# One-hot rows of slots in a graph network: formed by GpSimd from a slot table, one operation behind each gather

## What is computed

```python
edge_index = jnp.stack([src, dst])          # src, dst: 400000 each, sorted by dst
x = layernorm(x + gnn0(x, edge_index, edge_attr_4, edge_attr_8))

def sconv(x, src, dst, basis, wi, W, R, b):  # once in each of the three layers
    z = einsum('nc,kco->nko', x, W)          # 64 taps
    msg = sum over 8 corners of basis[:, s] * z[src, wi[:, s]]
    agg = segment_sum(msg, dst) / clip(cnt, 1)
    return agg + x @ R + b
```

## Time and profile before

| | |
|---|---|
| median of 3 timed runs | 15385.09 us (15372.33 to 15392.76) |
| span of the profiled execution | 20957.9 us |
| TensorE busy | 15299.0 us (73% of the span) |
| VectorE busy | 11387.0 us (54%) |
| GpSimd busy | 11380.3 us (54%), 12003 instructions |
| ScalarE busy | 3304.1 us (16%) |
| mean granted clock of TensorE | 0.788 of full speed |
| chain that ended last | TensorE 51%, another core or an unknown queue 28%, issue 14% |
| DMA | 353.06 MB, mean 17 GB/s |

### The profile page before, as it was taken

How to read it: one execution, slowest core, us unless ns; L and a number is a source line. 1 busy time by engine, 2 the same in 40 slices (tenths; PEclk the granted TensorE clock), 3 DMA queues, 4 the chain that set the end, 5 groups by cost and what they waited for, 6 DMA issues and landing times.

```text
span 20957.9 us, 179979 instructions
## 1 busy us (share of the span) xinstructions
PE 15299.0 (73%) x55111; PEld 8212.8 (39%) x55111; DVE 11387.0 (54%) x19145; ACT 3304.1 (16%) x4009; POOL 11380.3 (54%) x12003
## 2 busy tenths in 40 slices
PE   7788888888866767676666676667666676766676
PEld 3333333333333444443433343444443343434343
DVE  4556666656655555555545555555555555555555
ACT  1111111111111111111111111111111111111111
POOL 5445555555545555555545555555554555555554
PEclk7666666666678888888878888888887888888888
DMA  1000000000010000000010000000001000000000
GB/s 33 13 14 15 15 15 15 15 14 15 15 24 16 16 16 16 16 16 16 16 23 16 17 16 16 16 16 16 17 16 23 16 16 16 16 16 16 16 16 22
DMA packets 886190, 353.06 MB, mean 17 GB/s; under 512 B 604191, under 2 KB 877680, under 8 KB 885872
## 3 DMA queue, kind: packets, MB, share of 16 engines
q0 software_dynamic: 386208, 210.78, 5.9%
q1 hardware_dynamic: 329276, 112.29, 2.3%
q10 hardware_dynamic: 170644, 29.29, 0.8%
HBM read 314.88 MB, written 36.56 MB: 17 GB/s over the span
## 4 chain that ended last, share of the span: by engine, by line
PE 51%; another core or an unknown queue 28%; issue 14%; ACT 3%; DVE 3%; ACTq 1%; DMA 0%; POOL 0%; DVEq 0%; SPq 0%; POOLq 0%
PE ps L1547 17%; PE ps L1559 16%; PE ps L1459 5%; PE ps L1570 4%; PE ps L1475 3%; ACT big L792 2%; PE ps L1448 2%; PE ps L1442 2%; DVE big L1056 1%; PE ps L1432 1%; ACT big L710 1%; ACTq L802 1%; ACT big L700 0%; PE ps L1414 0%
## 5 line engine op out<-in xcount | busy, mean ns | idle before, releaser
L571 POOL DMA_INDIRECT xg<-x_rows,idx x8790 | 8316.4, 946 | 6310.6 <-DVE big L1254 3682.7
L1547 PE MATMUL ps<-big 128*128 128x256 f32 x18816 | 5050.5, 422 | 1286.7 <-ACT big L792 1250.4
L1237 DVE TENSOR_TENSOR big<-ps,onehot 128x1024 f32<-128x1024 f32 x2352 | 2864.7, 1218 | 5084.9 <-remote 3417.8
L1547 PEld LDWEIGHTS ps<-big 128*128 128x128 f32 x18816 | 3863.2, 211 | 3111.9 <-issue 2581.3
L571 POOL DMA_INDIRECT xg<-in_x,idx x3125 | 2974.6, 952 | 2806.5 <-DVE big L1026 1826.0
L1570 PE MATMUL ps<-big,w_taps 128*32 128x512 f32 x9408 | 1544.9, 734 | 3060.8 <-issue 2851.8
L792 ACT COPY big<-ps 128x1024 f32<-128x1024 f32 x2352 | 2353.5, 1013 | 8828.4 <-PE ps L1547 5318.7
L1559 PE MATMUL ps<-xw,big 128*128 128x512 f32 x8232 | 3671.5, 597 | 50.5 <-issue 23.2
L1459 PE MATMUL ps<-w,big 65*128 65x256 f32 x6272 | 2498.1, 541 | 126.9 <-DVE big L1056 85.6
L1559 PEld LDWEIGHTS ps<-xw,big 128*128 128x128 f32 x8232 | 1543.4, 190 | 2006.9 <-issue 1981.1
L1459 PEld LDWEIGHTS ps<-w,big 65*128 65x128 f32 x6272 | 1566.0, 267 | 1875.0 <-issue 1562.7
(11 more groups left out here) (139 smaller groups left out, 6620.8 us busy)
## 6 DMA issues: line engine op xcount, KB each, us to landing
xg<-x_rows,idx POOLq DMA_INDIRECT x8790
xg<-in_x,idx POOLq DMA_INDIRECT x3125
row_of<-pick_rows SPq DMA_DIRECT2D x294, 128.0 KB
agg_rows<-rts ACTq DMA_DIRECT2D x294, 64.0 KB
meta<-in_coord_t SPq DMA_DIRECT2D x294, 48.0 KB
big<-in_rad SPq DMA_DIRECT2D x196, 64.0 KB
meta<-meta_items SPq DMA_DIRECT2D x392, 32.0 KB
idx<-in_src_t SPq DMA_DIRECT2D x392, 16.0 KB
```

The costliest lines, as they stand in the source:

```text
L571: return nc.gpsimd.indirect_dma_start(out=dst_tile, out_offset=None, in_=table, in_offset=bass.IndirectOffsetOnAxis(ap=index, axis=0))
L1237: v.tensor_tensor(bm[:, ring], hat_outer[:, its].rearrange("p n c b -> p n (c b)").unsqueeze(3) .to_broadcast([P, 4, 16, J]), onehot[:, it ...
L1547: tr = nc.tensor.matmul(ps[:, 2 * (ch % 2) + r // 2, 256 * (r % 2):256 * (r % 2) + 256], xm[:, at].rearrange("p a c -> p (a c)"), bm[:, at ...
```

## The change

In the layers the one-hot rows are formed by GpSimd. Behind each gather it issues one TENSOR_SCALAR that compares the 16 slot numbers with the tile's slot, one number per partition; for tiles without a gather it issues the operation alone. That makes 32 operations of 128x16 a step, 9408 in the three layers. `onehot` gets two halves, one for each parity of steps, and the table has one channel of slots (`meta[:, par, 3]`) in place of two. The first part keeps its comparison on VectorE, without line 1038. GpSimd now waits for the step's table (`meta_loaded`) before its first gather, SyncE waits for the rows of two steps earlier (`onehot_ready`) before it loads over their table, and VectorE waits for the rows of a quarter before that quarter's first multiply. Making and storing the table takes three VectorE operations and one DMA less. `xt`, used between the layers, moves into the shared buffer `big`; the wide path is changed in the same way.

```diff
-    META = 9
+    META = 8
...
-        slot = sb("slot", [P, STEP])
-        onehot = sb("onehot", [P, STEP, CH])
+        onehot = sb("onehot", [P, 2, STEP, CH])
...
-            def load_meta(i, par, used, table, first, end):
+            def load_meta(i, par, used, table, first, end, made=0):
...
                 sp.sem_inc(loads_go, 1)
-                sp.dma_start(meta[:, par, 3:5, :], meta_items[:, ds(i, 1), 3:5, :].rearrange("p n c i -> p (n c) i")
+                if due(made):
+                    sp.wait_ge(onehot_ready, made)
+                    sp.sem_inc(loads_go, 1)
+                sp.dma_start(meta[:, par, 3:4, :], meta_items[:, ds(i, 1), 3:4, :].rearrange("p n c i -> p (n c) i")
                              ).then_inc(meta_loaded[par], 16)
...
-                    sp.dma_start(by_step[:, :, 3, :], quarter_t.rearrange("p (n i) -> p n i", i=STEP)
-                                 ).then_inc(meta_stored, 16)
-                    sp.dma_start(by_step[:, :, 4, :], place_t.rearrange("p (n i) -> p n i", i=STEP)
+                    sp.dma_start(by_step[:, :, 3, :], slot_t.rearrange("p (n i) -> p n i", i=STEP)
                                  ).then_inc(meta_stored, 16)
...
-            def gather_sources(table, phase, par, twice, group_free, rest=STEP, picked_in=()):
+            def gather_sources(table, phase, par, twice, group_free, rest=STEP, picked_in=(), with_hots=False):
                 pool.wait_ge(idx_loaded[par], 16 * phase * steps_of(path, par) + 8 * twice)
                 pool.sem_inc(gathers_go, 1)
+                if with_hots:
+                    pool.wait_ge(meta_loaded[par], 2 * loads(path, par, phase, twice))
+                    pool.sem_inc(gathers_go, 1)
                 for q in range(4):
                     if group_free:
                         pool.wait_ge(*group_free(q))
                         pool.sem_inc(gathers_go, 1)
                     for r in range(QUART):
                         s = QUART * q + r
-                        if s >= rest or q in picked_in and r == PICK:
-                            continue
-                        gather(xg[:, par, s, :], table, idx[:, par, s:s + 1]).then_inc(x_in[par][q], 16)
+                        if not (s >= rest or q in picked_in and r == PICK):
+                            gather(xg[:, par, s, :], table, idx[:, par, s:s + 1]).then_inc(x_in[par][q], 16)
+                        if with_hots:
+                            hot = nc.gpsimd.tensor_scalar(onehot[:, par, s, 0:J], slot_ids[:], meta[:, par, 3, s:s + 1],
+                                                          None, ALU.is_equal)
+                    if with_hots:
+                        hot.then_inc(onehot_ready, 1)
...
-                link(v.tensor_scalar(quarter_t.bitcast(I32), dst_i, NG.bit_length() - 1, None, ALU.arith_shift_right))
-                link(v.tensor_tensor(quarter_t, quarter_t.bitcast(I32), first_dst, ALU.subtract))
-                link(v.tensor_scalar(place_t.bitcast(I32), dst_i, NG - 1, None, ALU.bitwise_and))
-                link(v.tensor_copy(place_t, place_t.bitcast(I32)))
+                link(v.tensor_tensor(slot_t, dst_i, first_dst, ALU.subtract))
...
-                        v.scalar_tensor_tensor(slot[:], meta[:, par, 3, :], float(GROUP), meta[:, par, 4, :], ALU.mult, ALU.add
-                                               ).then_inc(dve_step, 1)
-                        at = at + MASKS
-                        dve.wait_ge(dve_step, at)
-
                         if due(i):
                             dve.wait_ge(deg_done, i)
-                        v.tensor_tensor(onehot[:, :, 0:J], slot[:].unsqueeze(2).to_broadcast([P, STEP, J]),
+                        v.tensor_tensor(onehot[:, 0, :, 0:J], meta[:, par, 3, :].unsqueeze(2).to_broadcast([P, STEP, J]),
                                         slot_ids[:].unsqueeze(1).to_broadcast([P, STEP, J]), ALU.is_equal
                                         ).then_inc(onehot_ready, 1)
...
-                v.scalar_tensor_tensor(slot[:], meta[:, par, 3, :], float(GROUP), meta[:, par, 4, :], ALU.mult, ALU.add
-                                       ).then_inc(dve_step, 1)
-                dve.wait_ge(dve_step, prior + 1)
...
-                v.tensor_tensor(onehot[:, :, 0:J], ids_ps.unsqueeze(1).to_broadcast([P, STEP, J]),
-                                slot[:].unsqueeze(2).to_broadcast([P, STEP, J]), ALU.is_equal).then_inc(dve_step, 1)
...
+                    if ch % 2 == 0:
+                        dve.wait_ge(onehot_ready, STEPS + 4 * n1 + ch // 2 + 1)
                     v.tensor_tensor(bm[:, ring], hat_outer[:, its].rearrange("p n c b -> p n (c b)").unsqueeze(3)
                                     .to_broadcast([P, 4, 16, J]),
-                                    onehot[:, its, 0:J].unsqueeze(2).to_broadcast([P, 4, 16, J]), ALU.mult)
+                                    onehot[:, par, its, 0:J].unsqueeze(2).to_broadcast([P, 4, 16, J]), ALU.mult)
```

More of the change, by code:

```diff
@@ L236, in graph_kernel @@
         picked, at = part(at, (J, CH))
+        assert at <= BIG
+        xt, at = part(TABLES_AT + 2 * NI, (2, BANK))
         assert at <= BIG
@@ L489, in l0_loads @@
                     load_indices(0, i + 1, 1 - par, twice)
-                load_meta(i, par, 0 if early and i < 2 else i - 1, sh_table, 5, META)
+                load_meta(i, par, 0 if early and i < 2 else i - 1, sh_table, 4, META)
                 load_carry(i - 1, 1 - par, 0 if early and i < 3 else i - 2)
@@ L648, in layer_gathers @@
                             else lambda q: (xm_ready[2 * q + 1], l * STEPS + i - 1))
-                    gather_sources(x_rows, l + 1, par, twice, free, padded if last else STEP, path.picks)
+                    gather_sources(x_rows, l + 1, par, twice, free, padded if last else STEP, path.picks, True)
                 for i in range(2):
@@ L684, in copy_block @@
                                ps[:, 1, :].rearrange("p (c n i) -> p c n i", c=4, n=4)).then_inc(item_out, 1)
[L685 to L687 removed]
+                nc.scalar.copy(src_t, ps[:, 2, 0:P]).then_inc(item_out, 1)
             if not path.narrow:
@@ L1011, in features @@
                     hv = xg[:, par, its, MUL:CH].rearrange("p n (u i) -> p n i u", i=3)
-                    sh0 = meta[:, par, 5, its]
-                    sh1 = meta[:, par, 6:9, its].rearrange("p i n -> p n i")
+                    sh0 = meta[:, par, 4, its]
+                    sh1 = meta[:, par, 5:8, its].rearrange("p i n -> p n i")
                     f_s = feat[:, its, :].rearrange("p n (s u) -> p n s u", s=4)
@@ L1393, in transpose_block @@
             def transpose_block(b):
-                pe.wait_ge(rows_ready, 3 * (b + 1))
+                pe.wait_ge(rows_ready, 2 * (b + 1))
                 if due(b):
-                    pe.wait_ge(item_out, 4 * b)
-                for c in range(5):
+                    pe.wait_ge(item_out, 3 * b)
+                for c in range(4):
                     nc.tensor.transpose(ps[:, c // 4, (c % 4) * P:(c % 4) * P + P], table_f[:, c * P:c * P + P],
                                         ident[:])
-                for c in range(5, META):
+                for c in range(4, META):
                     nc.tensor.transpose(ps[:, c // 4, (c % 4) * P:(c % 4) * P + P],
-                                        attr_r[:, (c - 2) * P:(c - 1) * P], ident[:])
-                nc.tensor.transpose(ps[:, 2, P:2 * P], src_f, ident[:]).then_inc(item_tr, 1)
+                                        attr_r[:, (c - 1) * P:c * P], ident[:])
+                nc.tensor.transpose(ps[:, 2, 0:P], src_f, ident[:]).then_inc(item_tr, 1)
             if not path.narrow:
@@ L1432, in l0_degrees @@
                 nc.tensor.matmul(ps[CH:2 * CH, 7, :].rearrange("p (s i) -> p i s", s=J), ones[:, 0:CH],
-                                 onehot[:, :, 0:J], start=True, stop=True, tile_position=(0, CH)).then_inc(deg_done, 1)
+                                 onehot[:, 0, :, 0:J], start=True, stop=True, tile_position=(0, CH)).then_inc(deg_done, 1)
             def first_layer(i, f):
@@ L1474, in item_sums @@
                         m = 2 * par + h
-                        tr = nc.tensor.matmul(ps[CH * m:CH * m + CH, SUMS[e % 2], :], onehot[:, 2 * q + h, :],
+                        tr = nc.tensor.matmul(ps[CH * m:CH * m + CH, SUMS[e % 2], :], onehot[:, 0, 2 * q + h, :],
                                               prod[:, q % 8, h, :], start=True, stop=True, tile_position=(0, CH * m))
```

72 lines of the change are left out of this document (31 added, 41 removed).

## The result

The changed kernel takes 18451.5 us (18444.48 to 18459.25 in 4 runs), the kernel before takes 15379.1 us (15372.33 to 15392.76 in 4 runs) beside it. The ratio is 1.1997, 95% interval 1.1982 to 1.2012: 3072 us slower. The forecast was 16786 us with a range up to 17915, so the sign was right and the time lay outside the range.

What follows compares the result with a forecast made beforehand. The prediction took GpSimd, issuing gathers nearly without a break, to bound the timed runs. 15385 us, plus 1411 for the added operations, less 10 for the first part, gave 16786 us, range 15350 to 17915.

Steps and rivals of the forecast that it cites:

- The bound, GpSimd: Whole kernel: the timed runs are GpSimd issuing gathers nearly without a break, 1.25 us apart.
- the floor of 15147 us: Whole kernel: time from GpSimd's gathers, totals, one wait, start and end alone, 98.5% of the measured median.
- the 31.5 us of the compute side: End of a layer: TensorE with its helpers needs 31.5 us a step, less than GpSimd's 37.5.
- Taking the pauses out: Every step: 14.2 us of pause, 5573 us in all, was taken to be in the profiled execution alone.
- the span hardly moves: Profile after: its span was expected within 1.5% of 20957.9 us, while the timed median grows.
- Terms (1) to (4): VectorE work removed in layers 0, removals in the first part -10 us, narrower tables 0, new waits 0.
- doesn't wait for long: Layers, VectorE's line 1237: its new wait for a quarter's last row was expected to be short and cost 0.
- Term (5): Layers, GpSimd: 9408 added operations behind gathers at 0.15 us each, mostly serial, +1411 us.
- full gap: Layers, GpSimd: each operation costs its own time and a 0.30 us gap, 0.40 in all, +3763 us; chance 0.08.
- Hidden: Layers, GpSimd: operations fit in the 0.30 us behind each gather, so not slower, 15375 us; chance 0.15.
- pipelined like a MEMSET: Layers, GpSimd: each operation costs 0.03 to 0.08 us, +282 to +753 us; chance 0.17.
- GpSimd isn't the bound: Timed runs: the 1.25 us spacing is stretched by profiling, VectorE's relief counts, 15095 to 15350 us; chance 0.04.

Runs made afterwards that it cites:

- The quiet trace: The kernel before, unchanged, run again for its profile on a chip without a pause in every step: 15362.8 us.
- the tables alone: The changed kernel with the comparison back on VectorE and no operations behind GpSimd's gathers: 15372.5 us, ratio 0.9997 to the kernel before.

## Why the prediction was right or wrong

**The bound, GpSimd: right.** The unbroken distance of 1.249, the floor of 15147 us and the 31.5 us of the compute side led to "GpSimd issues gathers nearly without a break". The quiet trace shows just that, and three times 200 us on VectorE changed nothing.

**Taking the pauses out: right in effect, wrong in its reason.** The prediction said that they are "in the profiled execution alone". They belong to some chips, where the timed runs have them too: 20696 to 21033 us. That the trace and the times ahead of the prediction came from different kinds of chip fits this, though no record names theirs. So "the span hardly moves" was wrong twice. The new profile is from a quiet chip (18449.1 us), and on a chip with pauses the span is 20338.4, 3.0% below the given 20957.9 where at most 1.5% was allowed. The reason given there, that 12.5 us of waiting in a step cover the added work, did hold: 32 x 0.33 = 10.6 us fit. That the pauses could go by it was not foreseen.

**Terms (1) to (4): right within the measurement.** VectorE's 255 us in the layers are worth 0, the tables and new waits 0. The start and the first part were taken at -10; the tables alone gave -5 us, within 15 us of 0 and of -10 alike. VectorE's first multiply does wait for GpSimd, 6465.5 us, against "doesn't wait for long". That is VectorE's spare time in another row and costs nothing, as the sum above closes without it.

**Term (5), the price of the operation: this is the step that failed.** The number of operations and "mostly serial" were right, c was not: 0.33 us instead of 0.15, 3083 us instead of 1411. The ends of the bound were 0 and 0.40, and c lies between them. The choice inside went wrong. It was made by two neighbours, a MEMSET on GpSimd (0.10) and a 128x16 copy on VectorE (0.18). The first is no neighbour: a MEMSET of the operation's own width adds 0.006 to 0.009 us behind a gather where the comparison adds 0.331. The second is another engine: GpSimd takes 0.29 to 0.31 us from one such operation's start to the next, where VectorE's copy takes 0.18. Both were recorded lengths, and the price is a distance between starts. With neither end excluded by a row, 0.08 to 0.27 held too much of the weight. The case of a full gap each got 0.08, though its 0.40 is as near to 0.33 as the forecast's upper end of 0.27 is.

**The rivals.** *Hidden* and *pipelined like a MEMSET* are what a MEMSET does (0.006 to 0.009 for one), and the comparison does not. *Full gap* had the better size and the wrong mechanism: the gap ahead of the gather isn't doubled but falls from 0.30 to 0.17. *GpSimd isn't the bound* is excluded on quiet chips. On chips with pauses it is the true one for the kernel before, and the 3% gain there has its sign, though not by VectorE's relief.

## What to carry to other kernels

Before work is moved to GpSimd, count its instructions and not their elements. Here a TENSOR_SCALAR costs 0.25 to 0.37 us behind a gather at any width from 1 to 32, so 9408 small ones cost 3.1 ms where VectorE's 294 wide ones cost nothing. Read the bound from start-to-start distances and not from busy shares, since GpSimd was 74% busy and fully bound. And where a profile's span and the timed runs disagree by a third, they may be of different chips: measure both kernels on one chip, and on more than one, since here the verdict turned from 1.20 to 0.97.

## What the runs showed of the hardware

- An indirect gather of 128 rows costs GpSimd 1.249 us start to start, 0.94 of it recorded as busy and 0.30 as issue. One MEMSET between two gathers adds only 0.006 to 0.009 us.
- A TENSOR_SCALAR of 128x16 on GpSimd costs 0.29 us in a row of eight and 0.33 between gathers. Of this the scalar from memory is 0.08 and the sixteen elements some 0.05. Whether VectorE is busy or idle beside it makes no difference (1.580 us either way).
- With comparisons between them, the gather is recorded as 1.03 us long in place of 0.94, and its gap as 0.17 in place of 0.30. The sum is what counts. That bears out the warning of the Trainium skill (Trace Analysis, "GPSIMD Engine Instruction") to go by starts.
- The same program takes 15.4 ms on two of the chips and 20.7 to 21.0 ms on three, with one wait for "remote" of some 12 us in each layer step, which by the kernel's order is a wait for TensorE's signal. It shrinks when gathers are issued 0.07 to 0.09 us further apart by MEMSETs, and is gone with one comparison between them (0.25 us and more). The cause was not found.
